# The last attention of a four-layer kernel: scores in three fp16 passes, probabilities divided on ScalarE

## The reference, cut to what matters

```
q = rms_norm(h @ wq) * q_norm_w        # 16 heads of 128, then rotated by position (cos, sin)
k = rms_norm(h @ wk) * k_norm_w        # 4 key heads, rotated; each serves 4 query heads
k_ctx = rms_norm(c @ wk_ctx) * k_norm_w   # not rotated
v, v_ctx = h @ wv, c @ wv_ctx
scores = q @ [k_ctx, k].T / sqrt(128) + causal mask on k
x = x + tanh(g) * (softmax(scores) @ [v_ctx, v]) @ wo
```

## Time and profile before

| | us |
|---|---|
| median of 3 runs | 3606.37 (3606.24 to 3606.59) |
| the profiled execution | 3601.69 |
| its span in the profile | 3599.9 |
| PE busy | 2964.1 (82%) |
| DVE busy | 2606.7 (72%) |
| ACT busy | 1641.7 (46%) |
| POOL busy | 872.3 (24%) |
| window 2250 to 3345, most of stage 6: PE busy | 1010 of 1095 |

### The profile page before, as it was taken

One profiled execution on the slowest core, in us unless ns is written; L12 is line 12 of the kernel. 1 busy time (PEld: TensorE's weight loads), 2 busy tenths in 40 slices (PEclk: granted clock), 3 DMA queues, 4 the chain that ended last, 5 costly groups with the idle time before them and its releaser, 6 DMA issues.

```text
span 3599.9 us, 50392 instructions
## 1 busy us (share of the span) xinstructions
PE 2964.1 (82%) x18610; PEld 1735.8 (48%) x18610; DVE 2606.7 (72%) x4530; ACT 1641.7 (46%) x2565; POOL 872.3 (24%) x1293
## 2 busy tenths in 40 slices
PE   3899899884668888578788745899999999998898
PEld 1343476663334444256566522444444444444565
DVE  4799769999756666588888874677777777776333
ACT  3000044444335555138778862444444444455343
POOL 2454200000000000015666682222222222221000
PEclk8899999997879999799989967999999999999999
DMA  7222022212211010200000021000000000012000
GB/s 263 83 79 76 27 59 71 59 48 71 54 24 30 22 24 10 97 30 2 1 1 2 4 87 53 7 7 1 7 7 1 7 7 1 7 37 61 13 17 17
DMA packets 52642, 132.51 MB, mean 37 GB/s; under 512 B 6416, under 2 KB 19536, under 8 KB 51152
## 3 DMA queue, kind: packets, MB, share of 16 engines
q1 hardware_dynamic: 43216, 96.11, 8.7%
q10 hardware_dynamic: 9216, 33.56, 3.1%
HBM read 119.03 MB, written 4.19 MB: 34 GB/s over the span
## 4 chain that ended last, share of the span: by engine, by line
PE 37%; DVE 17%; issue 10%; ACT 7%; POOL 1%; DMA 0%; DVEq 0%; SPq 0%; POOLq 0%; ACTq 0%
PE psum L1093 11%; PE psum L2392 3%; PE psum L1904 3%; PE psum L2433 3%; ACT area_g L1982 2%; PE psum L2417 2%; DVE area_c L2035 2%; PE psum L1918 2%; PE psum L1315 2%; PE psum L1334 2%; PE psum L2402 2%; DVE area_a L1651 2%; PE psum L1294 1%; PE psum L1939 1%; DVE small L2671 1%
## 5 line engine op out<-in xcount | busy, mean ns | idle before, releaser
L1982 ACT ACTIVATE area_g<-area_a 128x2048 bf16<-128x2048 f32 x156 | 310.6, 1995 | 43.7 <-DVE area_a L2053 30.2
L1904 PE MATMUL psum<-area_c,ident_bf 128*128 128x128 bf16 x3584 | 245.1, 232 | 100.3 <-DVE area_c L2035 100.3
L2671 DVE TENSOR_REDUCE small<-psum 128x1 f32<-128x384 f32 (+1 forms) x256 | 159.1, 622 | 188.5 <-PE psum L2393 188.5
L515 PE MATMUL psum<-area_b,area_g 128*128 128x512 f32 x640 | 281.2, 599 | 16.0 <-DVE area_g L464 14.4
L172 POOL TENSOR_TENSOR rstd<-mean_var,eps_col 128x2 f32<-128x2 f32 x65 | 16.3, 251 | 1139.9 <-DVE mean_var L581 528.4
L1904 PEld LDWEIGHTS psum<-area_c,ident_bf 128*128 128x128 bf16 x3584 | 227.8, 105 | 129.6 <-DVE area_c L2035 122.9
L659 PE MATMUL psum<-xT_high,area_a 128*128 128x256 f16 x1024 | 237.8, 280 | 1.4 <-DVE xT_low L596 1.4
L659 PE MATMUL psum<-xT_low,area_a 128*128 128x256 f16 x1024 | 237.4, 280 | 0.0
L2392 PE MATMUL psum<-area_b,stage 128*128 128x512 f32 (+1 forms) x512 | 234.5, 540 | 0.0
L2543 ACT ACTIVATE area_g<-psum 128x384 f16<-128x384 f32 (+1 forms) x256 | 139.3, 544 | 168.7 <-PE psum L2402 166.7
L515 PEld LDWEIGHTS psum<-area_b,area_g 128*128 128x128 f32 x640 | 121.3, 192 | 175.2 <-issue 164.6
(11 more groups left out here) (394 smaller groups left out, 7548.6 us busy)
## 6 DMA issues: line engine op xcount, KB each, us to landing
stage<-in_w ACTq DMA_DIRECT2D x24, 512.0 KB, 4.3
stage<-in_w SPq DMA_DIRECT2D x24, 512.0 KB, 3.7
area_g<-in_toeplitz SPq DMA_DIRECT2D x32, 256.0 KB, 3.5
area_b<-in_ctxT SPq DMA_DIRECT2D x16, 512.0 KB, 3.9
area_b<-area_b SPq DMA_DIRECT2D x24, 256.0 KB, 3.7
x_stream<-in_x SPq DMA_DIRECT2D x4, 1024.0 KB, 8.9
area_c<-in_ctxT SPq DMA_DIRECT2D x4, 1024.0 KB, 15.4
area_g<-in_ctx SPq DMA_DIRECT2D x8, 512.0 KB, 5.2
```

Source lines behind the costliest of these rows:

```text
L515: last = nc.tensor.matmul(psum[:, 4 * par + m, :], toep[:, par, (m - k) * P:(m - k + 1) * P], kv[:, par, k, :], start=(k == 0), stop=(k == m))
L1904: last = nc.tensor.matmul(psum[:, 1, t_ * P:(t_ + 1) * P], identb[:, :], above5[:, t_, c * P:(c + 1) * P], start=(c == 0), stop=(c == KE - 1))
L1982: nc.scalar.activation(junk5[t_], z5[b % 3][:, t_, :], ACT.Sign, bias=fine5[:, par, t_:t_ + 1], scale=-1.0, accum_out=signs5[:, t_:t_ + 1] ...
L2671: nc.vector.tensor_reduce(nmax6[:, n % 2:n % 2 + 1], psum[:, 2 + n % 2, 0:nk], AX.X, ALU.min).then_inc(sig("nmax6_ready"), 1)
```

## The change

- Queries and keys are kept as fp16 high and low halves. `scores` runs three fp16 matmuls (high x high, low x high, high x low) and the mask matmul as before. ACT takes the high half out of PSUM (`query_out`, new `key_high`), DVE the low half (new `query_low`, `key_out`). The signals `qT6_ready` and `kT6_ready` are now given by DVE's low halves.
- Rotation tables and key weights are multiplied by factors that bring queries and keys to fp16's range; the scale back (`s6`) is applied in the exponential and, in a new second instruction of `maximum`, to the bias.
- The division by the row's sum moves from DVE to ACT: `normalise` is now an ACT copy with a scale, and DVE keeps the reciprocal (`invert`), first in each head's turn.
- The context is loaded to views of its own (`ctx6`) in the same memory. Semaphores `x4_added` and `x6_added` become one (`attention_added`), `hid7_ready` is joined to `hid_ready`, with counts moved; the diff leaves these lines out.

```diff
@@ -2188,7 +2188,8 @@
         w3_o = [view(area_c, 0, [KE, D], F16), view(area_a, 32768, [KE, D], F16)]
-        kT6 = view(area_b, 16384, [2 * 4 * G3, P]).rearrange("p (a n g) k -> p a n g k", a=2, n=4)
+        kT6 = view(area_b, 16384, [2 * 4, 2 * G3, P], F16).rearrange("p (a n) (v g) k -> p a n v g k", a=2, v=2)
+        ctx6 = [view(area_b, 16384 + 8192 * n, [KD, S]) for n in range(2)]
         v6 = view(area_a, 16384, [2 * 4, 2, D], F16).rearrange("p (a n) v d -> p a n v d", a=2)
...
@@ -2196,7 +2197,7 @@
         oT6 = stage[:, 0, 512:1024].bitcast(F16).rearrange("p (v h q) -> p v h q", v=2, h=4)
-        qT6 = stage[:, 1, :].rearrange("p (a h q) -> p a h q", a=2, h=4)
+        qT6 = stage[:, 1, :].bitcast(F16).rearrange("p (a v h q) -> p a v h q", a=2, v=2, h=4)
         p6 = xn[:, 1]
...
@@ -2234,9 +2237,18 @@
             dc.step(nc.vector.tensor_copy(key_w6[:, :], norm_w6[:, 1, :]))
+            dc.link(nc.vector.scalar_tensor_tensor(out=abs_w6, in0=norm_w6, scalar=-1.0, in1=norm_w6, op0=ALU.mult, op1=ALU.max))
+            dc.link(nc.vector.tensor_reduce(top6w, abs_w6, AX.X, ALU.max))
+            dc.link(nc.vector.tensor_scalar(top6w[:, 0:1], top6w[:, 0:1], ROW_TOP * SC6, 1e-6, ALU.mult, ALU.max))
+            dc.link(nc.vector.tensor_scalar(top6w[:, 1:2], top6w[:, 1:2], ROW_TOP, 1e-6, ALU.mult, ALU.max))
+            dc.step(nc.vector.reciprocal(S1("rq6"), top6w[:, 0:1]))
+            dc.step(nc.vector.reciprocal(S1("rk6"), top6w[:, 1:2]))
+            dc.step(nc.vector.scalar_tensor_tensor(out=S1("s6"), in0=top6w[:, 0:1], scalar=-1.0 / (NORM * NORM), in1=top6w[:, 1:2],
+                                                   op0=ALU.mult, op1=ALU.mult))
 
             dc.settle()
-            dc.step(nc.vector.tensor_scalar(rope6[:, 0], rope6[:, 0], -SC6, None, ALU.mult))
+            for tab, r, c in ((rope6[:, 0], "rq6", -SC6 * NORM), (rope6[:, 1], "rk6", NORM), (key_w6[:, :], "rk6", NORM)):
+                dc.step(nc.vector.tensor_scalar(tab, tab, S1(r), c, ALU.mult, ALU.mult))
             dc.step(nc.vector.tensor_scalar(tri6[:, :], tri_raw, -1.0, None, ALU.mult))
...
@@ -2389,7 +2401,9 @@
                     pe.wait_ge(sig("p6_ready"), n - 1)
-                nc.tensor.matmul(psum[:, 2 + n % 2, 0:nk], qT6[:, u % 2, h, :], kT6[:, b % 2, 0:nk // P, g, :], start=True, stop=False)
+                for qp, kp in ((0, 0), (1, 0), (0, 1)):
+                    nc.tensor.matmul(psum[:, 2 + n % 2, 0:nk], qT6[:, u % 2, qp, h, :], kT6[:, b % 2, 0:nk // P, kp, g, :],
+                                     start=(qp + kp == 0), stop=False)
                 nc.tensor.matmul(psum[:, 2 + n % 2, nk - P:nk], identb[:, :], tri6[:, :], start=False, stop=True).then_inc(sig("s6_ready"), 1)
...
@@ -2519,7 +2533,13 @@
                 act.wait_ge(sig("qT6_ps_ready"), u + 1)
-                nc.scalar.activation(qT6[:, u % 2], psum[:, 7, :].rearrange("p (h q) -> p h q", h=4), ACT.Copy).then_inc(sig("qT6_ready"), 1)
+                nc.scalar.activation(qT6[:, u % 2, 0], psum[:, 7, :].rearrange("p (h q) -> p h q", h=4),
+                                     ACT.Copy).then_inc(sig("qT6_high_ready"), 1)
+
+            def key_high(b, j):
+                act.wait_ge(sig("kT6_ps_ready"), 4 * b + j // 2 + 1)
+                nc.scalar.activation(kT6[:, b % 2, key_block(j), 0], psum[:, 0, :].rearrange("p (g n) -> p g n", g=G3),
+                                     ACT.Copy).then_inc(sig("kT6_high_ready"), 1)
 
...
@@ -2532,7 +2552,13 @@
                 nc.scalar.activation(p6[:, n % 2, 0:nk], psum[:, 2 + n % 2, 0:nk], ACT.Exp, bias=nmax6[:, n % 2:n % 2 + 1],
-                                     scale=-1.0, accum_out=sum6[:, n % 4:n % 4 + 1]).then_inc(sig("p6_ready"), 1)
+                                     scale=S1("s6"), accum_out=sum6[:, n % 4:n % 4 + 1]).then_inc(sig("p6_ready"), 1)
+
+            def normalise(n):
+                nk = NK6[place(n // 4)[2]]
+                act.wait_ge(sig("rsum6_ready"), n + 1)
+                nc.scalar.activation(p6[:, n % 2, 0:nk], p6[:, n % 2, 0:nk], ACT.Copy,
+                                     scale=rsum6[:, n % 4:n % 4 + 1]).then_inc(sig("pn6_ready"), 1)
 
...
@@ -2559,6 +2585,7 @@
                 if j % 2:
+                    key_high(0, j - 1)
                     value_in(0, j)
...
@@ -2577,9 +2604,12 @@
                 exps(n)
+                normalise(n)
                 if h == 0:
                     if u:
                         out_in(u - 1)
+                if h == 1 and w % 2 and b + 1 < B:
+                    key_high(b + 1, w - 1)
                 if h == 1 and w == 1 and b + 1 < B:
...
@@ -2635,8 +2665,14 @@
             def key_out(b, j):
-                dve.wait_ge(sig("kT6_ps_ready"), 4 * b + j // 2 + 1)
-                nc.vector.tensor_copy(kT6[:, b % 2, key_block(j)], psum[:, 0, :].rearrange("p (g n) -> p g n", g=G3)).then_inc(sig("kT6_ready"), 1)
+                dve.wait_ge(sig("kT6_high_ready"), 4 * b + j // 2 + 1)
+                nc.vector.tensor_tensor(kT6[:, b % 2, key_block(j), 1], psum[:, 0, :].rearrange("p (g n) -> p g n", g=G3),
+                                        kT6[:, b % 2, key_block(j), 0], ALU.subtract).then_inc(sig("kT6_ready"), 1)
+
+            def query_low(u):
+                dve.wait_ge(sig("qT6_high_ready"), u + 1)
+                nc.vector.tensor_tensor(qT6[:, u % 2, 1], psum[:, 7, :].rearrange("p (h q) -> p h q", h=4), qT6[:, u % 2, 0],
+                                        ALU.subtract).then_inc(sig("qT6_ready"), 1)
 
...
@@ -2668,14 +2704,13 @@
                 dve.wait_ge(sig("s6_ready"), n + 1)
-                nc.vector.tensor_reduce(nmax6[:, n % 2:n % 2 + 1], psum[:, 2 + n % 2, 0:nk], AX.X, ALU.min).then_inc(sig("nmax6_ready"), 1)
-
-            def normalise(n):
-                nk = NK6[place(n // 4)[2]]
+                lo = nmax6[:, n % 2:n % 2 + 1]
+                dc.link(nc.vector.tensor_reduce(lo, psum[:, 2 + n % 2, 0:nk], AX.X, ALU.min))
+                nc.vector.tensor_scalar(lo, lo, S1("s6"), -1.0, ALU.mult, ALU.mult).then_inc(sig("nmax6_ready"), 1)
+
+            def invert(n):
                 dve.wait_ge(sig("p6_ready"), n + 1)
-                r = rsum6[:, n % 4:n % 4 + 1]
-                dc.link(nc.vector.reciprocal(r, sum6[:, n % 4:n % 4 + 1]))
-                nc.vector.tensor_scalar(p6[:, n % 2, 0:nk], p6[:, n % 2, 0:nk], r, None, ALU.mult).then_inc(sig("pn6_ready"), 1)
+                nc.vector.reciprocal(rsum6[:, n % 4:n % 4 + 1], sum6[:, n % 4:n % 4 + 1]).then_inc(sig("rsum6_ready"), 1)
 
...
@@ -2723,6 +2758,8 @@
                 key_end(0, j)
+                if j == 2:
+                    query_low(0)
                 key_out(0, j)
...
@@ -2736,6 +2773,7 @@
                 b, w, t_, g = place(u)
+                invert(n)
                 if h == 0:
...
@@ -2747,7 +2785,6 @@
                     value_low(b + 1, w)
-                normalise(n)
                 if h == 0 and u + 1 < UNITS:
...
@@ -2757,6 +2794,8 @@
                         query_end(u + 1)
+                if h == 3 and u + 1 < UNITS:
+                    query_low(u + 1)
                 if h == 3:
```

More of the change, by code:

```diff
@@ L1220, in bias @@
             def bias(i, st):
-                pool.wait_ge(sig("x4_added"), nth(i, st, 1, 1))
+                pool.wait_ge(sig("attention_added"), nth(i, st, 1, 1))
                 xt = X[:, i * 4 + st, :]
@@ L1438, in step @@
                             if u == 5:
-                                need(pe, "x4_added", nth(i, st, 1, 0))
+                                need(pe, "attention_added", nth(i, st, 1, 0))
                                 values(i, st, 0)
@@ L1664, in x_add @@
                 nc.vector.scalar_tensor_tensor(out=xt, in0=psum[:, 1, :], scalar=gates[:, 2:3], in1=xt,
-                                               op0=ALU.mult, op1=ALU.add).then_inc(sig("x4_added"), 1)
+                                               op0=ALU.mult, op1=ALU.add).then_inc(sig("attention_added"), 1)
             dve.wait_ge(sig("tables_loaded"), 64)
@@ L2206, in build @@
         norm_w6 = xn[:, 1, 0, 0:2 * P].rearrange("p (w d) -> p w d", w=2)
+        abs_w6 = xn[:, 1, 1, 0:2 * P].rearrange("p (w d) -> p w d", w=2)
+        top6w = small6[:, 28:30]
         tri6 = sb("tri6", [P, P], BF16)
@@ L2210, in build @@
         PV6 = 32768.0
+        ROW_TOP = 1.001 * float(P) ** 0.5
         XN_TOP = 1.001 * float(D) ** 0.5
@@ L2222, in sp_stage6 @@
                     sp.wait_ge(sig("s6_ready"), 32 * (b - 1))
-                sp.dma_start(kT6[:, b % 2, 0:2].rearrange("p n g k -> p (n g k)"),
-                             t["ctxT"][:, :, b, :]).then_inc(sig("ctx_part_loaded"), 16)
+                sp.dma_start(ctx6[b % 2], t["ctxT"][:, :, b, :]).then_inc(sig("ctx_part_loaded"), 16)
                 if b == 0:
@@ L2427, in project_out @@
                     if g == 0 and u:
-                        pe.wait_ge(sig("x6_added"), u // G3)
+                        pe.wait_ge(sig("attention_added"), NTILES + u // G3)
```

(17 more changed lines are left out.)

## The result

The changed kernel takes 3720.93 us (3720.53 to 3723.83, 4 runs) against 3606.48 for the kernel before in the same comparison: ratio 1.032, interval 1.0308 to 1.0332, slower by 114 us. Its profiled execution has a span of 3718.7 us against 3599.9. It was forecast at 3714.

A forecast was written before the change was run, and what follows sets the result against it. PE was taken as the bound (128.35 of 137 us per batch), with heads as relays. +13.5 us for seven batches (+94.5), +11 last batch, +3 start: +108.5 on 3606.4 gives 3714; range 3675 to 3755.

The forecast's parts named there:

- The two new waits: PE waits for DVE's query_low before each query projection; in odd units key_out waits for ACT's key high half, 0.73 us later.
- the extra operand: The exponential on ACT now reads its scale from a tile: 0.09 us more each, with 0 and 0.1 as ends.
- The start of the stage: Start of the last attention: four key copies on ACT (4 x 0.6) and query_low add 3 us.
- The larger tables: Some 3 us more on DVE, before its 3.25 us wait for PE; counted at nothing, +3 if that cover is gone.
- The +1.7 of the unit with the scaling: One even unit per batch scales the input on DVE under head 1; late third exponential and ACT division make +1.7 us.
- the 2.25 for odd units of 384 keys: Two odd units per batch at 384 keys: late key copies delay maximum, exponential and query_low, +2.25 us each.
- ACT's division: The division moved from DVE (0.487 us per head) to ACT: 0.71 us, with 0.60 to 0.75 as ends.
- the second instruction of `maximum`: Small DVE multiplication of 0.17 us after the reduction; ACT's exponential starts 0.21 to 0.23 us later after the scores.
- The term of 0.1 us won at `out_low`: Where DVE's low half gates PE's third pair of output-projection matmuls: at best 0.1 us gained, 0.3 per batch.
- stall 0.8 us ahead of the transposes of head 2: Odd units: PE waits 0.8 us for ACT's late division; the same stall covers the key projection's wait for key_out.
- the rival of a falling clock: New PE gaps halve the TensorE clock for a tenth of the stage: +100 us on top, 3815; chance 0.05.
- too short: The last batch has PE gaps of its own at clock 1.00, so the new gaps are too short to lower it.

The follow-up runs named there:

- experiment 4: Changed kernel (result: kernel 4) with query_low under head 2, and key transposes and key high half earlier: 3599.87 us, ratio 0.9986 to the kernel before.
- experiment 8: Kernel with both moves of experiment 4, without the scale back of the scores (wrong-sized scores): 3570.33 us, ratio 0.9905 to the kernel before.
- Experiment 2: Changed kernel with only the key transposes and ACT's key high half moved earlier under head 1: 3691.76 us, ratio 1.024 to the kernel before.
- experiment 5: Kernel before with only the division moved from DVE to ACT, invert first on DVE: 3595.73 us, ratio 0.9978 to the kernel before.
- experiment 6: Changed kernel with only the division put back on DVE, behind value_low and ahead of query_low: 3742.10 us, ratio 1.038 to the kernel before.
- experiment 7: Kernel with both moves of experiment 4 and the division back on DVE: 3601.68 us, ratio 0.9989 to the kernel before.

## Why the prediction was right, and where its terms were off

**The mechanism.** The two new waits stood where the prediction put them, and taking both away (experiment 4) gave back 121 us, more than the 114 lost. The chain of the earlier trace rows, with 0.09 for the extra operand, had the query projection 1.10 us later; measured 1.16 (2.46 against 1.30).

**The sum, term by term.** Units of one batch, first value to first value:

| unit | before | after | more | forecast |
|---|---|---|---|---|
| even, 384 keys (two) | 15.40, 16.05 | 16.65, 17.29 | 1.25, 1.24 | 1.1 |
| even, 512 | 16.70 | 17.60 | 0.90 | 0.8 |
| even, 512, with the scaling | 17.78 | 19.47 | 1.69 | 1.7 |
| odd, 384 (two) | 17.33, 17.31 | 19.86, 19.17 | 2.53, 1.86 | 2.25 |
| odd, 512 (two) | 17.89, 18.11 | 20.26, 20.70 | 2.37, 2.59 | 2.3 |
| batch | 136.57 | 151.00 | 14.4 | 13.5 |

Seven batches, from the first values of the stage, make 100.6 us (the first is 14.2 longer, the others 14.4 or nearly; forecast 94.5), and the seven steps behind them 9.6 (11 for eight): up to 1.8 each where the signs of weights stand in ACT's queue, 0.6 to 1.0 in the others. The start of the stage took 5.0 us more (forecast 3): PE waits 2.35 us for the query's low half where it waited 0.37 for ACT's copy, and 1.42 instead of 0.79 for each of three keys. The larger tables cost nothing, as assumed: DVE needs 5.9 us for them instead of 3.8, and its wait for PE behind them shrinks from 3.25 to 1.10. The stage's first projection came 1.9 us later, but DVE had begun the tables later by the same 1.9, so that part comes from ahead of the changed code and was not followed. The clock took 1.7 (below). 100.6 + 9.6 + 5.0 + 1.9 + 1.7 = 118.8, the difference of the spans.

Two agreements are luck. The +1.7 of the unit with the scaling was put down without a working. And the 2.25 for odd units of 384 keys is right as a mean only, with 2.53 and 1.86 behind it. The difference is an instruction that the prediction did not look at: from the second batch on, the first odd unit adds a finished tile to x (`x_add`) on DVE under head 0, ahead of the maximum and `out_low`. In the first batch this unit has no such tile, and takes 19.17 us like the other one. PE's wait for `out_low` in it, with `x_add` (second batch) and without (first batch):

```profile
2432.84 0.74 DVE L2746 SCALAR_TENSOR_TENSOR x_stream<-psum,scalars,x_stream 128x512 f32<-128x512 f32 x1
...
2436.47 0.60 PE L2447 MATMUL psum<-area_c,stage 128*128 128x512 f16 x2 [1.72 <-DVE stage L2726]
```
```profile
2285.11 0.60 PE L2447 MATMUL psum<-area_c,stage 128*128 128x512 f16 x2 [1.07 <-DVE stage L2726]
```

**Sizes.** ACT's division was put at 0.71 us and took 0.722; the exponential was put at +0.09 and took +0.10; the second instruction of `maximum` was put at 0.17, by an instruction on four columns with a constant, and took 0.214. The term of 0.1 us won at `out_low` was wrong in sign: that wait grew by 8 us in 600. The prediction said that the second instruction eats the shorter scores' 0.21 us; with the extra operand of the exponential it costs 0.37 in a unit of kernel 4 (experiment 8).

**In odd units** one step went another way. The prediction let PE stall 0.8 us ahead of the transposes of head 2 and called `key_out` covered by it. The timeline has 0.44 at the projection under head 2 (2662.93; in odd units it is that of the values, not the keys, and waits for `key_out` because it writes the same bank), and some 0.3 at the transposes (2666.96, 0.35 behind the mask matmul where it was 0.06). The end of the relay is the same: the query projection starts 9.97 us after the key's transposes instead of 7.47, the 2.5 of the prediction. Experiment 2 gave 29 us where such a unit was priced at 0.8, so the key chain is worth 1.1.

**The rule on multiplications.** "ScalarE: Activation LUTs" in the Trainium skill, "Rules for kernel authors", wants them on VectorE. By duration that holds here (0.487 against 0.722). By the kernel's time it doesn't: experiment 5 is faster without following it, and experiment 6 slower by 21 us for following it (8 of them the clock's), since the queue of DVE, and what stands behind, decided. In kernel 4 the place made no difference (experiment 7).

**The TensorE clock** stayed at 1.00 in all full batches, gaps of 1.81 us included, as the one in the timeline above. It fell once, for the last values of the stage, behind gaps of 1.70, 1.10 and 0.69 us:

```profile
3452.10 4.45 PE L2431 MATMUL psum<-area_g,area_a 128*128 128x512 f16 x12 [0.69 <-ACT area_g L2569]
```

The same twelve matmuls took 2.76 us before; the granted clock in 3454 to 3457 is 0.63, between the two levels. That is 1.7 us of the 119, so the rival of a falling clock is out as the cause. But the prediction's "too short" holds for these gaps by little: in experiment 6 these gaps are 0.16 us longer, and six of fourteen are followed by a fall.

**Left open.** How the 0.37 us of experiment 8 divide between the small instruction, its wait and the extra operand was not tried, nor which gaps make the clock fall.

## What to carry to other kernels

When a signal is handed from one engine to another, look at where in the new engine's queue it is given and what stands ahead: here a buffer that ACT freed under head 2 was freed by DVE under head 3, behind an instruction that waits for the next exponential, and 0.7 us of work became 1 us of waiting or more in most units (91.7 us in 62). An operation moved off a busy engine should be priced by the queue it leaves and the queue it joins, not by its own length. And a wait that ends the same way in every unit (here 0.7 us ahead of the values) is worth more than faster matmuls: moving existing work into it gave 41 to 47 us, while three fp16 passes, priced at 48 us of PE's time, left kernel 4 only 0.14% faster. Look at the granted clock beside every such comparison: a small change of a gap can add to a kernel's time what its queue does not explain (experiment 6).

## What had not been expected of the hardware

An instruction on one column of 128 partitions whose scale is read from a tile took 0.214 us on DVE, 0.04 more than the one with constants of the earlier trace rows, which has four columns. Six of fourteen gaps of PE of 1.97 us were followed by a clock of 1.2 GHz for six to eight matmuls of 512 columns, and none of fourteen gaps of 1.80 or 1.81 us at the same places (experiment 6 and the changed kernel). And the same division on DVE, 384 columns, took 0.98 us where it started within 0.04 us of POOL's multiplication (2444.35 and 2444.39 in the kernel before), 0.42 beside the other heads; that POOL is the cause was not tried.
